# A graph kernel in four phases: its first phase rearranged, and key/value rows of 2048 bytes

## What is computed

```python
enh = node_features + 0.1 * query_emb[None, :]
Q, K, V = ((enh @ W + b).reshape(N, H, D) for W, b in ((Wq, bq), (Wk, bk), (Wv, bv)))
mod_k = K[src] + 0.2 * rel_w[edge_relations][:, None, :]
scores = jnp.einsum('ehd,ehd->eh', Q[dst], mod_k) / D ** 0.5
w = softmax of scores over the edges of one dst
agg = jax.ops.segment_sum(w[:, :, None] * V[src], dst, num_segments=N)
msgs = jnp.where(deg[:, None, None] > 0, agg, V)
out = msgs.reshape(N, H * D) @ Wo + bo
```

## Time and profile before

| | us |
|---|---|
| median of 3 runs | 5471.56 |
| fastest, slowest run | 5470.32, 5476.66 |
| span of the profiled execution | 7316.7 |
| TensorE busy in it (matmuls) | 5674.8 |
| VectorE, ScalarE, GpSimd busy | 4006.7, 2651.7, 3696.3 |

### The profile page before, as it was taken

One profiled execution on the slowest core, in us unless ns is written; L12 is line 12 of the kernel. 1 busy time (PEld: TensorE's weight loads), 2 busy tenths in 40 slices (PEclk: granted clock), 3 DMA queues, 4 the chain that ended last, 5 costly groups with the idle time before them and its releaser, 6 DMA issues. The chain is left out here.

```text
span 7316.7 us, 142121 instructions
## 1 busy us (share of the span) xinstructions
PE 5674.8 (78%) x41507; PEld 4231.9 (58%) x41507; DVE 4006.7 (55%) x12046; ACT 2651.7 (36%) x9038; POOL 3696.3 (51%) x3942
## 2 busy tenths in 40 slices
PE   5767777777777777777797688888878788787888
PEld 3356666666666666666553355556656565555666
DVE  4345555555555555555685455555555555555553
ACT  3434444444444444444321133332323233333334
POOL 2255555555555555555344655555555555555550
PEclk8889999989999999998898788888889888889988
DMA  5576666666666666667565444443434434344431
GB/s 137 159 196 172 175 175 172 173 176 175 173 173 175 173 174 174 172 171 166 128 203 163 117 118 118 116 123 108 124 109 121 118 109 122 110 119 119 116 115 34
DMA packets 615779, 1055.40 MB, mean 144 GB/s; under 512 B 150117, under 2 KB 399547, under 8 KB 615504
## 3 DMA queue, kind: packets, MB, share of 16 engines
q0 software_dynamic: 233984, 716.19, 35.8%
q1 hardware_dynamic: 232374, 181.93, 8.3%
q10 hardware_dynamic: 149210, 155.22, 7.3%
HBM read 913.94 MB, written 142.26 MB: 144 GB/s over the span
## 5 line engine op out<-in xcount | busy, mean ns | idle before, releaser
L1709 POOL DMA_INDIRECT rm_xg<-tx_rows,rm_idx x1875 | 1785.1, 952 | 1413.2 <-PE rm_pa L1740 823.1
L800 POOL DMA_INDIRECT at_kv<-kv_rows,at_idx x1760 | 1673.5, 951 | 1559.9 <-PE at_p_o L929 1028.3
L1740 PE MATMUL rm_pa<-rm_xg,rm_oh 128*126 128x256 f32 x3750 | 1246.9, 451 | 557.6 <-DVE rm_acc L2067 435.3
L2067 DVE SCALAR_TENSOR_TENSOR rm_acc<-rm_acc,rm_kp,rm_pa 126x256 f32<-126x256 f32 x1875 | 897.6, 479 | 858.4 <-PE rm_pa L1740 450.0
L1740 PEld LDWEIGHTS rm_pa<-rm_xg,rm_oh 128*126 128x126 f32 x3750 | 711.9, 212 | 942.2 <-DVE rm_acc L2067 526.2
L929 PE MATMUL at_p_o<-at_kv,at_pt 128*64 128x129 f32 x7040 | 750.5, 293 | 630.0 <-issue 549.9
L985 ACT ACTIVATE at_ex<-at_p_s,at_ntop 128x128 f32<-128x128 f32 x1760 | 503.2, 369 | 1377.2 <-DVE at_ntop L1059 1245.0
L929 PEld LDWEIGHTS at_p_o<-at_kv,at_pt 128*64 128x64 f32 x7040 | 491.9, 142 | 854.2 <-issue 838.9
L1051 DVE TENSOR_REDUCE at_cmax<-at_p_s 128x4 f32<-128x512 f32 x440 | 303.8, 690 | 1101.9 <-DMA rows<-pre_rows_b 1055.1
L909 PE MATMUL at_p_s<-at_hot,at_own 128*64 128x128 f32 x7040 | 764.2, 292 | 40.8 <-issue 39.8
L912 PE MATMUL at_p_s<-at_kt,at_own 128*64 128x128 f32 x7040 | 743.0, 283 | 67.1 <-issue 66.7
(11 more groups left out here) (250 smaller groups left out, 7364.4 us busy)
## 6 DMA issues: line engine op xcount, KB each, us to landing
at_row<-rows ACTq DMA_DIRECT2D x440, 128.0 KB
agg_rows<-rm_acc SPq DMA_DIRECT2D x300, 126.0 KB
rm_st<-agg_rows ACTq DMA_DIRECT2D x75, 504.0 KB
rm_srow<-agg_rows ACTq DMA_DIRECT2D x75, 504.0 KB
tx_rows<-up_tx SPq DMA_DIRECT2D x49, 768.0 KB, 3.6
rm_xg<-tx_rows,rm_idx POOLq DMA_INDIRECT x1875
at_kv<-kv_rows,at_idx POOLq DMA_INDIRECT x1760
sums<-at_acc SPq DMA_DIRECT2D x196, 64.5 KB
```

What stands on the lines that cost most here:

```text
L800: eng.indirect_dma_start(out=kv[j][:, c, :], out_offset=None, in_=t.kv, in_offset=bass.IndirectOffsetOnAxis(ap=idx[:, o:o + 1], axis=0),). ...
L1709: eng.indirect_dma_start(out=xg[:, q % XR, :], out_offset=None, in_=t.tx, in_offset=bass.IndirectOffsetOnAxis(ap=idx[:, q % IR:q % IR + 1] ...
L1740: eng.matmul(p_a[q % BANKS][0:WR, 0:D], oh[:, q % OR, :], xg[:, q % XR, :], start=True, stop=True).then_inc(summed, 1)
L2067: v_.scalar_tensor_tensor(acc[:, q % AR, :], acc[:, (q - 1) % AR, :], kp[0:WR, q % AR:q % AR + 1], p_a[q % BANKS][0:WR, 0:D], ALU.mult, AL ...
```

## The change

- The relation weights (64x64) are loaded as whole rows, twice side by side, turned by one TensorE transpose and scaled by ScalarE. Before, two DMAs read them transposed from DRAM, and GpSimd scaled them.
- SP pads dst first; the first two tiles of x are loaded before the other three arrays are padded. GpSimd gathers the heads of rows once dst alone is padded, and clears `fresh0` after that.
- VectorE reads gathered integers in place, without first making float copies. Both `starts` come before the first `tile_counts`, and TensorE's slots move.
- GpSimd's queue, no longer SP's, stores the two lists and the seven tables. SP, no longer ScalarE's queue, stores r. Some tables have 16-bit numbers.
- A kv row is [128 values, 256 keys, 128 values], 2048 bytes, and ScalarE copies it with one instruction. The columns of ones are set once in attention's buffers, around the gathered row.
- Attention's first indices are copied before the masks are built. The update loads sums in one DMA, and own values in one.

```diff
-KV = D + 2 * VP
+KV = 2 * D
+KVW = KV + 32
+VAT, KAT = (15, 400), 144
...
-                        link(v.tensor_copy(found[:, :], found_i[:, at, :]))
-                        link(v.tensor_scalar(junk[:, :], found[:, :], bounds[:, L, g:g + 1], 0.0,
+                        link(v.tensor_scalar(junk[:, :], found_i[:, at, :], bounds[:, L, g:g + 1], 0.0,
...
                 starts(0)
+                starts(1)
                 tile_counts(0)
                 first_edges(0)
-                starts(1)
...
-                    eng.memset(kv[par][:, :], 1.0).then_inc(setup, 1)
...
-                tsc(rel[:, :], relc[:, :], 0.2, None, ALU.mult).then_inc(setup, 1)
-                eng.memset(t.fresh0[:, :], 0.0).then_inc(iota_done, 1)
-                eng.wait_ge(iota_done, 5)
-                eng.memset(t.fresh0[:, 0:1], -2.0 * BIG).then_inc(iota_done, 1)
-                eng.wait_ge(arrays_padded, 16 * 8)
+                eng.wait_ge(dst_padded, 32)
...
-                eng.wait_ge(x_turned, NB - 2)
-                eng.memset(x[0][:, :], 0.0).then_inc(x_zero, 1)
+                eng.wait_ge(dve.sem, plan["rows_b"])
+                for k in range(2):
+                    eng.dma_start(t.rows0[k, :].rearrange("(g p e) -> p g e", p=P, e=C0),
+                                  rows_b[:, :, k, :]).then_inc(rows0_out, 16)
+                eng.wait_ge(dve.sem, plan["taken", 1, G1 - 1])
+                for k, of in enumerate((src1, row1, keep, need, ends, slot)):
+                    rows = P if k < 3 else 1
+                    eng.dma_start(t.tables1[k][0:rows, :], of[0:rows, :]).then_inc(tables_out, 16)
...
-                STARTS, SPREAD, RANGES, ROWS = (6, 18), 22, (36, 63), (46, 72)
+                STARTS, SPREAD, RANGES, ROWS = (8, 9), 21, (35, 63), (44, 72)
...
+                eng.transpose(p_r[0][:, 0:R64], relr[:, :, :].rearrange("t e d -> t (e d)"), t.ident[0:R64, 0:R64]
+                              ).then_inc(rel_ps, 1)
...
-                    eng.dma_start(relc[HD * e:HD * e + HD, :], a["L0_gnn_rel_w"].rearrange("t d -> d t"),
-                                  allow_slow_non_contiguous=True).then_inc(w_in, 16)
+                    eng.dma_start(relr[:, e, :], a["L0_gnn_rel_w"]).then_inc(w_in, 16)
...
-                    act(kv[par][:, 0:D], p_kv[par][:, 0:D], ACT.Copy).then_inc(kv_done, 1)
-                    for e in range(2):
-                        at = (HD + 1) * e
-                        act(kv[par][:, D:KV].rearrange("p (k c) -> p k c", k=2)[:, :, at:at + HD],
-                            p_kv[par][:, D:2 * D].rearrange("p (k c) -> p k c", k=2)[:, :, HD * e:HD * e + HD],
-                            ACT.Copy).then_inc(kv_done, 1)
+                    act(kv[par][:, :], p_kv[par][:, :], ACT.Copy).then_inc(kv_done, 1)
...
+                eng.wait_ge(rel_ps, 1)
+                act(rel[:, :], p_r[0][:, 0:R64], ACT.Copy, scale=0.2).then_inc(rel_done, 1)
...
+                    eng.wait_ge(rt_done, i + 1)
+                    eng.sem_inc(t.sp_on, 1)
+                    eng.dma_start(t.r0[bass.ds(i * 4 * R64, 4 * R64), :].rearrange("(w p) c -> p w c", p=R64),
+                                  rt[par][:, :, :]).then_inc(out_r[par], 16)
+                load(0, 0, True, P)
+                load(1, 1, True, P)
+                pad_arrays()
...
-                            out=kv[j][:, c, :], out_offset=None, in_=t.kv,
+                            out=kv[j][:, c, 16:16 + KV], out_offset=None, in_=t.kv,
...
+                for b in range(2):
+                    set_rows(2 * b, b)
...
+                for i in range(U):
+                    v.memset(kv[i][:, :, VAT[0]:VAT[0] + 1], 1.0)
+                    ins = v.memset(kv[i][:, :, VAT[1] + VE - 1:VAT[1] + VE], 1.0)
+                ins.then_inc(cleared, 1)
...
+                    eng.dma_start(sums[b][:, 0:H * VP], t.sums0[bass.ds(i * P, P), :]).then_inc(x_in[b], 16)
```

More of the change, by code:

```diff
@@ L117, in prepare_phase @@
         keep = s.sb("keep", [P, G1 * P])
-        need = s.sb("need", [P, G1 * P], I32)
-        ends = s.sb("ends", [P, NW], I32)
+        need = s.sb("need", [P, G1 * P], U16)
+        ends = s.sb("ends", [P, NW], U16)
         before = s.sb("before", [P, NW], I32)
@@ L587, in tile @@
                         eng.wait_ge(rt_done, i - 1)
+                    else:
+                        eng.wait_ge(rel_done, 1)
                     for k in range(2):
@@ L676, in load @@
                         eng.wait_ge(x_turned, i - 1)
-                    if rows < P:
-                        eng.wait_ge(x_zero, 1)
                     eng.dma_start(x[par][0:rows, :], a["x"][bass.ds(i * P, rows), :]).then_inc(x_in[par], 16)
@@ L690, in store @@
                                   qs[par][:, :, :, :, :].rearrange("p w k e n -> p w (k e n)")).then_inc(out_q[par], 16)
-                each(eng, load)
+                    eng.wait_ge(rt_done, i + 1)
[5 more added lines that the diff above has]
+                pad_arrays()
+                with eng.Fori(1, NB // 2 - 1) as k:
+                    load(k * 2, 0, False, P)
+                    load(k * 2 + 1, 1, False, P)
+                load(NB - 3, 0, False, P)
+                load(NB - 2, 1, False, P)
+                load(NB - 1, 0, False, N - (NB - 1) * P)
                 store(NB - 2, 1)
                 store(NB - 1, 0)
-                eng.wait_ge(dve.sem, plan["rows_b"])
-                for k in range(2):
-                    eng.dma_start(t.rows0[k, :].rearrange("(g p e) -> p g e", p=P, e=C0),
-                                  rows_b[:, :, k, :]).then_inc(rows0_out, 16)
-                eng.wait_ge(dve.sem, plan["taken", 1, G1 - 1])
-                for k, of in enumerate((src1, row1, keep, need, ends, slot)):
-                    rows = P if k < 3 else 1
-                    eng.dma_start(t.tables1[k][0:rows, :], of[0:rows, :]).then_inc(tables_out, 16)
-                eng.dma_start(t.tables1[6][:, :], ubase[:, :, :].rearrange("p u e -> p (u e)")).then_inc(tables_out, 16)
                 for par in range(2):
@@ L720, in attend_phase @@
         FLOOR = -float(2 ** 90)
-        kv = [s.sb(f"kv{i}", [P, CH, KV]) for i in range(U)]
+        kv = [s.sb(f"kv{i}", [P, CH, KVW]) for i in range(U)]
         idx = s.sb("idx", [P, U * CH], I32)
@@ L1135, in update_phase @@
         zero = s.sb("zero", [P, D])
-        sums = [s.sb(f"sums{i}", [P, 2 * (VP + 3)]) for i in range(R)]
+        sums = [s.sb(f"sums{i}", [P, 2 * MASS]) for i in range(R)]
         xb = [s.sb(f"xb{i}", [P, D]) for i in range(R)]
@@ L1506, in relate_mix_phase @@
         keep = s.sb("keep", [P, G1 * P])
-        need = s.sb("need", [1, G1 * P // 5], I32)
-        ends = s.sb("ends", [1, NW], I32)
+        need = s.sb("need", [1, G1 * P // 5], U16)
+        ends = s.sb("ends", [1, NW], U16)
         slot = s.sb("slot", [1, NW], I32)
```

143 lines of the change are left out of this document (74 added, 69 removed).

## The result

The changed kernel takes 5448.55 us (median of 4 runs, 5443.24 to 5451.53) against 5473.09 for the kernel before on the same chip (4 runs): a ratio of 0.9954, 95% interval 0.9942 to 0.9966, so 24.5 us less. In a later group of runs on a chip of the same pace it was 5447.21 against 5474.29: 0.9952 (0.9938 to 0.9965), 27.1 us less. The forecast was 5456; the sum of its terms was -15.0. The intervals reach some 7 us to either side, so 2 or 3 us between two such numbers are no difference.

The account below looks back on a forecast made before the run. TensorE was taken as the limit in attention and update, leaving gains to the first stage and its borders: -12.4 - 11.3 - 3.3 + 8 + 4 = -15.0 us from 5471.56, forecast 5456, range 5418 to 5480.

Parts of the forecast that it names:

- The start: Before the first tile: weights in whole rows and x behind one padded array bring the first transpose sooner, -12.4 us.
- Rival 4: First tile: the start does not move because x or weights are late behind padded arrays; 5466 us, chance 0.15.
- VectorE's lists: First stage: dropped copies and earlier lookups all lie under VectorE's own wait of 48.3 us; value 0.
- The end of the stage: First stage's close: table stores on GpSimd's queue lie beside tiles, so attention starts sooner, -11.3 us, range -9 to -12.
- The head of attention: Attention's beginning: first indices copied before the masks, so the first gather comes sooner; -3.3 us, range -2 to -4.
- The loop that pays: First stage's tile loop: r's added slot on SP's queue delays x; +8 us, between 0 and 23.
- Rival 1: Tile loop: r in SP's queue eats the gain through TensorE's wait for x; +22 us, 5494, chance 0.12.
- The gather bursts: First stage while GpSimd issues index gathers: tiles crawl, nearest to no change; +4 us, from -20 to +26.
- rival 2: Gather bursts: they shrink because earlier lists break up the second burst less; 5433 us, chance 0.17.
- the rule cited there: Gather bursts: DMA engines take turns among queue rows, so r on SP's row costs 26 us; sum +7, 5479.
- Rows of 2048 bytes: Attention's gathers: 58 us of transfer saved at most, hidden while TensorE is the limit; value 0, range 0 to -58.
- rival 3: Attention: limited by gathers outside the trace, so half of the 58 us is won; 5427 us, chance 0.13.

Follow-up runs that it names:

- e1: Kernel before with only loaded wait-bound counters narrowed to 16-bit integers: 5470.95 us, ratio 0.9999.
- e2: Kernel before with 16-bit counters and the nine stores of rows and tables on GpSimd's queue instead of SP's: 5470.59 us, ratio 0.9999.
- e3: Kernel before with 16-bit counters and relation weights loaded in whole rows, turned by TensorE, array order kept: 5460.24 us, ratio 0.9981.
- e4: Kernel before with 16-bit counters, weights turned on TensorE and row and table stores on GpSimd's queue: 5461.59 us, ratio 0.9983.
- e11: Changed kernel run again unaltered, as control at the usual pace: 5447.21 us, ratio 0.9952 to the kernel before.
- e10: Changed kernel with the second layer's tables stored only after the last x tile is turned: 5439.55 us, ratio 0.9938 to the kernel before.
- e12: Changed kernel with tables stored after the last x tile and the last x load cut into 96 and 10 rows: 5440.24 us, ratio 0.994.
- e5_after: Changed kernel unaltered, on the slower chip: 7319.62 us, ratio 0.9994 to the kernel before there.
- e8: Changed kernel with kv rows of 2056 bytes again, on the slower chip: 7328.37 us, ratio 0.9994 to the kernel before there.

## Why the prediction was right, and where it was not

The direction was right and the size short (-15.0 against -24.5 and -27.1). Three terms of the sum were off, and one gain was in no term: the end of the stage was worth 5.7 us less than forecast, the loop and the bursts cost nothing instead of 12, and 40 tiles took 7.4 us less. The first error and the others have opposite signs; that the forecast came as near as it did is in part luck.

- **The start**, -12.4: measured -11.6 (23.5, the mean of e1 and e2, to 11.9). Right, but with the wrong one last: the prediction had the weights there at 9 us and x at 10.5; the weights came at 11.3, 2.3 us late, and x was not waited for. Behind them came GpSimd's two small operations, which the prediction had beside the transpose, and so the first tile started at 11.94 instead of 10.6. The order of the arrays was worth some 6.2 of the 11.6, as e3's wait for x tells. Rival 4 named this place, and it was the weights and not x that came late.
- **VectorE's lists**, 0: they end sooner (the stores can start at 231.4 us, against 238.1 in e4), but the first tile is 6 us sooner too, and no stage shows a gain that would be theirs alone. Not tried alone.
- **The end of the stage**, -11.3: the close became 12.5 us shorter (26.5 to 14.0), as argued, -9 to -12 nearly. The step that failed is "the table stores on GpSimd's queue lie beside tiles". The work beside them was taken as cover because another engine issues it; but three stores of 960 KB fill the same DMA engines that load x (331 and 359 GB/s), and x has little slack: TensorE waits for it in 21 of 40 tiles even without them (e11). The last four tiles took 6.9 us more. Net -5.6 in the changed kernel, -5.0 in e2 against e1 and -1.4 in e4 against e3. e10 shows the cause: stores moved past the last x bring attention's start 5.5 us forward. The Trainium skill (DMA: Bandwidth & Descriptors, Rules for kernel authors) says it in a line: DMAs from SP, ScalarE and GpSimd share the same 16 engines, and spreading them only saves issue time. The trace agrees, with 3.70 us of waiting for x at 331 GB/s.
- **The head of attention**, -3.3: the first gather follows 1.09 us after attention's start, where it was 4.39; attention is 3.0 us shorter (2312.8 to 2309.8). Right for the first gather. But that gather's issue now takes 2.18 us instead of 0.95 and ends 0.13 us after the 16 mask copies that VectorE makes beside it, so the second one comes 3.57 us after attention's start instead of 5.65 (e1): 2.1 us of the 3.3 are left to the gathers behind it. No run here was made to find why it is longer.
- **The loop that pays**, +8: measured 0 (199.7 and 201.9 us against 203.2 and, in e10 and e12 with r on SP's queue too, 201.3 and 200.5). The step that failed is the balance: the slot's delay of x was counted (at 0.6 us a tile; it is 1.0, and yet costs only 3 to 5 us of waits in 40 tiles), and of what ScalarE is spared only "one 128x512 copy instead of three" was; the 0.63 us by which the issue of r held ScalarE in each tile was left out, and TensorE's wait of 4.4 us for `qs` goes with it. Rival 1 falls with this.
- **The gather bursts**, +4, and rival 2: there is no stall. A profile with 1.34 times the time of the runs was taken for a picture of them; it was one of another pace, in which TensorE stands still for 28.4 us in one piece in the first burst (34.9 in e5_after). By the prediction's own sign this part was wrong: the first burst was to hold 3 tiles, and not 5, and it holds 11 in the changed kernel (52.5 to 106.8 us). The prediction knew the ratio, and its terms of issues and landings carried over one to one, as it said; those that were stalls did not. What the rule cited there would cost in the bursts (26 us) is not seen either: with r on SP's queue 40 tiles take 199.7 to 201.9 us.
- **Rows of 2048 bytes**, 0: the value is right, its reason is not. The transfer per MB fell 3.4%, attention's length did not follow. The prediction had it hidden "while TensorE is the limit"; at the usual pace TensorE waits 243 us for gathers, which is rival 3's condition, and GpSimd's issuing leaves no room, 2171 of 2309 us, which is what stood "against" that rival. So the 0 was right by another argument than the one that it was given; that the issuing is what holds attention is read from these shares and was not tried by a run.

What is not in the sum: 40 tiles took 209.2 and 207.1 us in e1 and e2 and 199.7 to 203.2 in the seven others, some 7 us less, and e3 and e4 have this with nothing changed but the start and the stores. The same 784 matmuls kept TensorE busy for 184.6 and 180.9 us there (clock 0.97, 0.98), 179.8 and 178.2 in e3 and e4 (0.99, 1.00). So part is clock: TensorE is busy 4.2 us less in the changed kernel's two profiles than in e1's and e2's (178.5 and 182.8 us in the mean), and its granted clock is at the lower level, 1.2 GHz, for 13.7 and 6.8 us of these 40 tiles in e1 and e2, for 3.4 us or not at all in e3, e4 and the changed kernel. The other 3 us are idle time. Whether the later start causes either, and whether two profiles a side are enough to say so, stays open. The terms as measured are -11.6 - 7.4 + 6.9 - 12.5 - 3.0 = -27.6.

## What to carry to other kernels

Work that is moved to another engine's queue is off that engine only: a bulk store still takes the DMA engines, so it belongs where no load with a deadline lies behind it, here after the last x tile, worth 5 to 8 us. When a DMA issue moves from one engine's queue to another's, count both sides: the queue that is longer, and the engine that is no longer held. Before a stall in a profile is priced, look whether the profiled execution keeps the pace of the runs; if it does not, take its issues and landings, and not its stalls, and ask anew which engine is the limit: here it was another one at the other pace.

## What the runs showed of the hardware

Chips differ: the kernel before took 7328 us on the chip of e5 to e8 and 5471 to 5474 us on the others. On the slower one waits grow that the trace can put down to no engine of the core ("remote", "issue"), above all while GpSimd issues gathers (waits of 57 to 120 us in e5_after: us in total, times, longest):

```profile
DVE pre_sorted_start L324 <- remote: 53.1, 1, 53.1
...
ACT pre_qs L637 <- remote: 34.8, 2, 26.2
...
PE pre_pr L589 <- issue: 7.6, 1, 7.6
```

What holds them is not told by the trace, and no run here was made to find it.

A wait of TensorE can be dearer than it looks: after the wait of 3.70 us for x that ended at 237.80 us, the granted clock of the next 6 us was 0.74, and the two transposes there took 0.69 us where the next tile's took 0.44; after the wait of 4.99 us at the end they took 0.69 us too. A load of 106 rows of 1 KB, with hardly anything beside it, kept the DMA engines at 0.11 of their time.
